# Where the causal mask is applied to the exponentials: mask products on TensorE, or a select on GpSimd, with values in pairs of heads and moved stack reads

## The reference

```python
x = x + attn(layernorm(x), Wq, Wk, Wv, Wo)            # 16 heads of 8, rotary, causal
x = x + xattn(layernorm(x), ctx, W_kv, W_q, W_proj, b) # 16 heads of 8, no mask
x = x + ffn(layernorm(x), gate, w1, b1, w2, b2)        # 8 experts, top 2 per sequence

attn = jnp.einsum('bhqd,bhkd->bhqk', q, k) * scale
attn = jnp.where(causal, -jnp.inf, attn)
attn = jax.nn.softmax(attn, axis=-1)
out = jnp.einsum('bhqk,bhkd->bhqd', attn, v)
```

## Time and profile before

| | |
|---|---|
| median of 3 runs | 200.97 us (200.36 to 201.46) |
| the profiled execution, its own time | 200.95 us |
| its span, first to last instruction | 199.2 us |
| mean granted TensorE clock | 0.947 of 2.4 GHz |
| TensorE busy / VectorE / ACT / GpSimd | 84% / 71% / 53% / 26% of the span |
| TensorE by line, chain that ended last | values L914 11%, second scores L893 9%, first scores L868 8% |
| mask products L898 | 12.1 us busy (overlapping), 48 of them |

### The profile page before, as it was taken

One profiled execution on the slowest core, in us unless ns is written; L12 is line 12 of the kernel. 1 busy time (PEld: TensorE's weight loads), 2 busy tenths in 40 slices (PEclk: granted clock), 3 DMA queues, 4 the chain that ended last, 5 costly groups with the idle time before them and its releaser, 6 DMA issues.

```text
span 199.2 us, 4411 instructions
## 1 busy us (share of the span) xinstructions
PE 166.8 (84%) x1500; PEld 116.1 (58%) x1508; DVE 140.7 (71%) x545; ACT 104.8 (53%) x222; POOL 52.3 (26%) x103
## 2 busy tenths in 40 slices
PE   0686195699599979989998998998998899799994
PEld 0343184485466755755764655654665556598984
DVE  2789299897347899799799889888968346525020
ACT  2132021257147656566566666766676657793451
POOL 7810005668800070030030030010115107126050
PEclk9999669589769999999999999999999999999999
DMA  5817660058227503322321321300340350170720
GB/s 150 238 35 175 164 173 18 3 148 184 70 82 196 184 25 104 110 69 58 109 82 49 98 95 35 90 0 3 113 130 3 100 143 0 17 224 26 229 66 26
DMA packets 23842, 19.05 MB, mean 96 GB/s; under 512 B 2364, under 2 KB 21820, under 8 KB 23100
## 3 DMA queue, kind: packets, MB, share of 16 engines
q1 hardware_dynamic: 22908, 17.79, 31.9%
q10 hardware_dynamic: 912, 0.98, 2.0%
HBM read 12.54 MB, written 2.49 MB: 75 GB/s over the span
## 4 chain that ended last, share of the span: by engine, by line
PE 50%; DVE 19%; DMA 15%; SPq 5%; issue 4%; POOL 3%; ACT 2%; POOLq 0%; DVEq 0%; ACTq 0%
PE psV L914 11%; PE psB L893 9%; PE psA L868 8%; DMA stackQ<-maxT 6%; DMA stackQ<-scratch 4%; DVE masked L623 4%; PE psA L958 4%; PE psM L923 3%; PE psA L975 3%; DMA stackK<-hid 3%; PE psV L975 3%; PE psM L933 3%; DVE stats L554 2%; DVE negmax L629 2%; SPq L402 2%
## 5 line engine op out<-in xcount | busy, mean ns | idle before, releaser
L753 ACT ACTIVATE E<-psB 128x512 f32<-128x512 f32 x112 | 62.3, 595 | 37.3 <-PE psB L893 15.7
L868 PE MATMUL psA<-stackK,stackQ 72*128 72x256 bf16 (+1 forms) x256 | 44.4, 277 | 11.8 <-DMA stackK<-hid 5.5
L893 PE MATMUL psB<-stackQ,stackK 74*128 74x256 bf16 (+1 forms) x256 | 42.2, 264 | 4.6 <-DMA stackQ<-maxT 3.8
L623 DVE CUSTOM_DVE_ANT_0 masked<-psA,row_mask 128x128 bf16<-128x128 f32 (+1 forms) x128 | 36.8, 352 | 11.8 <-PE psA L868 11.7
L629 DVE TENSOR_REDUCE negmax<-psA 128x2 f32<-128x512 f32 x64 | 39.7, 677 | 0.0
L868 PEld LDWEIGHTS psA<-stackK,stackQ 72*128 72x128 bf16 x256 | 23.0, 105 | 21.5 <-DMA stackQ<-scratch 8.6
L914 PE MATMUL psV<-E,V 128*9 128x256 f32 (+1 forms) x512 | 30.9, 359 | 0.2 <-ACT E L753 0.2
L893 PEld LDWEIGHTS psB<-stackQ,stackK 74*128 74x128 bf16 x256 | 22.0, 100 | 12.5 <-DMA stackQ<-maxT 5.6
L468 POOL TENSOR_SCALAR rstd<-mv 128x2 f32<-128x2 f32 x12 | 2.8, 236 | 89.1 <-DVE mv L558 88.9
L914 PEld LDWEIGHTS psV<-E,V 128*9 128x9 f32 x512 | 11.0, 90 | 14.4 <-issue 7.9
L761 ACT ACTIVATE oT<-psV 128x256 f32<-128x256 f32 x32 | 12.3, 384 | 7.9 <-PE psV L914 7.2
(11 more groups left out here) (111 smaller groups left out, 247.0 us busy)
## 6 DMA issues: line engine op xcount, KB each, us to landing
stackK<-scratch SPq DMA_DIRECT2D x18, 192.0 KB
stackQ<-hid SPq DMA_DIRECT2D x36, 64.0 KB
w1s<-w_dram SPq DMA_DIRECT2D x8, 258.0 KB, 2.8
w2s<-w_dram SPq DMA_DIRECT2D x8, 256.0 KB, 3.7
stackQ<-scratch SPq DMA_DIRECT2D x3, 576.0 KB
stackK<-hid SPq DMA_DIRECT2D x18, 64.0 KB
scratch<-hid SPq DMA_DIRECT2D x4, 192.0 KB, 3.7
scratch<-parts_ctx SPq DMA_DIRECT2D x4, 192.0 KB, 4.7
```

The source lines that it names most:

```text
L623: last = dve.tensor_tensor_reduce(out=masked[:, bank, i * keys:(i + 1) * keys], in0=scores[:, i, 0:keys], in1=row_mask[:, S - keys:S], sca ...
L753: act.activation(dst, psB[:, bank].rearrange("p (h q) -> p h q", h=dst.shape[1]), ACT.Exp, scale=SCALE).then_inc(b_taken, 1)
L868: last = pe.matmul(psA[:, bank, i * keys:(i + 1) * keys], stackQ[0:ROWS, b, h, t * P:(t + 1) * P], stackK[0:ROWS, b, h, 0:keys], start=Tru ...
L893: last = pe.matmul(psB[:, bank, i * n:(i + 1) * n], stackK[:, b, h, t * P:(t + 1) * P], stackQ[:, b, h, q0:S], start=(s == 1 or i == 0), s ...
```

## The change

- The mask products of the second pass go, and `mask16T` with them. Instead GpSimd sets the forbidden exponentials to 0 in `E`, two selects per self group: after unit 1 (keys 0 to 127) and after unit 2 (keys 128 to 255), each over 4 heads x 128 columns. The value products wait for both (`e_masked`).
- Values in pairs: heads are grouped as `heads_of(g)`, so two groups that follow each other hold the even and the odd heads of 8. Weights are 18 columns (the head's 9 and 9 zeros, or the reverse), and both groups add into one `psV` without a copy between. ACT copies after each second group; `o_turn` has 4 transposes into one bank, one reciprocal and one product.
- `max_rows` is split: TensorE's transpose (`max_turn`) stays behind the units of its half; VectorE's and SyncE's part (`max_rows`) moves ahead of the units of that half.
- The reads and writes of the stacks are separate steps for keys and queries; those of batch 2 come earlier, those of batch 3 and of the cross keys lie behind the row maxima in SyncE's queue.
- `q_cross`'s split goes from VectorE to an ACT copy and four GpSimd pieces (`q_split`); `k_split` is cut into four steps, a half apart; adding the projection bias is a step of its own (`add_bias`).
- `masked` has 2 buffers instead of 3.

```diff
@@ plan()
+    put(7, "max_turn", 0, 0)
     put(7, "max_rows", 0, 0)
...
-    put(9, "stack_write", 0, 2)
-    put(10, "stack_read", 0, 2)
-    put(14, "stack_write", 0, 3)
+    put(6, "stack_write", 0, 2, 1)
+    put(9, "stack_write", 0, 2, 0)
+    put(9, "stack_read", 0, 2, 1)
+    put(10, "stack_read", 0, 2, 0)
+    put(13, "stack_write", 0, 3, 1)
+    put(14, "stack_write", 0, 3, 0)
+    put(16, "stack_read", 0, 3, 1)
+    put(16, "stack_read", 0, 3, 0)
     for b in range(NB):
-        put(16 + 3 * b, "k_split", 1, b)
-        put(17 + 3 * b, "stack_write_k", 1, b)
+        for n in range(4):
+            put(14 + 4 * b + n, "k_split", 1, b, n)
+        put(17 + 4 * b, "stack_write_k", 1, b)
...
         if j > 0:
-            put(n + 2 * NG, "max_rows", s, b)
-        if j == 1:
-            put(n + 2 * NG + 1, "stack_read", 0, 3)
+            row_of[n + 2 * NG] = (s, b)
...
         if s == 0:
-            put(m, "stack_read_k", 1, b)
+            put(n + 24, "stack_read_k", 1, b)
             put(m + 5, "q_cross", 1, b)
             put(m + 5, "stack_fill", 1, b)
+            for n, later in enumerate((5, 5, 6, 6)):
+                put(m + later, "q_split", 1, b, n)
+            put(m + 7, "add_bias", 1, b)
...
+        if half in row_of:
+            order.append(("max_rows", *row_of[half]))
         order += [step for _, step in sorted(units, key=lambda unit: unit[0])]
+        if half in row_of:
+            order.append(("max_turn", *row_of[half]))
...
+def heads_of(g):
+
+    k, j = divmod(g, 2)
+    return [k * 2 * GH + 2 * i + j for i in range(GH)]
@@ GpSimd
-                    then(pool.memset(mask16T[:, :, :], 0.0))
-                    causal(mask16T, -1)
+                    pool.memset(v_pairs[:, :, VC:2 * VC], 0.0).then_inc(v_init, 1)
...
+                if kind == "scores_exp" and s == 0 and st["u"] >= 1:
+                    pool.wait_ge(b_taken, unit + 1)
+                    t = st["u"] - 1
+                    diagonal = E[:, (job * NG + g) % 3, :, t, t * P:(t + 1) * P]
+                    pool.affine_select(out=diagonal, in_=diagonal, compare_op=ALU.is_ge, fill=0.0, base=0,
+                                       pattern=[[0, GH], [1, P]], channel_multiplier=-1).then_inc(e_masked, 1)
+                if kind == "q_split":
+                    if g == 0:
+                        for bank, k in use[("q_cross", s, b)]:
+                            pool.wait_ge(misc_taken[bank], k)
+                    split(rot[:, b % 2, 0, 0], parts[:, b, 0], parts_q[b], g)
@@ VectorE
-                if kind == "q_cross":
-                    bank, k = misc[0]
...
-                    for t, (bank, k) in enumerate(misc):
-                        dve.wait_ge(misc_full[bank], k)
...
+                    bank, k = misc[0]
+                    dve.wait_ge(misc_full[bank], k)
...
+                    then(dve.reciprocal(r, o[:, :, :, HD]))
@@ ACT
+                if kind == "q_cross":
+                    bank, k = misc[0]
+                    act.wait_ge(misc_full[bank], k)
+                    act.wait_ge(parts_q_self[2 + b] if b < 2 else parts_q[b - 2], NPART)
+                    act.activation(rot[:, b % 2, 0, 0], psM[:, bank, 0:S], ACT.Copy).then_inc(misc_taken[bank], 1)
...
-                if kind == "values":
+                if kind == "values" and g % 2 == 1:
@@ TensorE
-                    if s == 0:
-                        blocks = psB[:, bank].rearrange("p (h q) -> p h q", h=len(heads))[:, :, 0:P]
-                        last = pe.matmul(blocks, ident16[:, :], mask16T[:, 0:len(heads), :], start=False, stop=True,
-                                         skip_group_check=True)
...
-                    else:
-                        pe.wait_ge(v_taken, grp)
+                    elif g % 2 == 0:
+                        pe.wait_ge(v_taken, grp // 2)
...
-                    pe.wait_ge(b_taken, b_units_until(grp))
+                    if s == 0:
+                        pe.wait_ge(e_masked, 2 * (grp + 1))
+                    else:
+                        pe.wait_ge(b_taken, b_units_until(grp))
+                    j = g % 2
...
+                            last = pe.matmul(psV[i * VW:i * VW + 2 * VC, q0:S], V[:, s, b, t, h // 2, j * VC:(j + 2) * VC],
+                                             E[:, grp % 3, i, t, q0:S], start=(j == 0 and t == 0),
+                                             stop=(j == 1 and t == 1), skip_group_check=True,
+                                             tile_position=(0, i * VW))
```

More of the change, by code:

```diff
@@ L53 @@
 VC = HD + 1
+NPAIR = NG // 2
 SCALE = float(HD) ** -0.5
@@ L72, in plan @@
 def plan():
-    extra = {}
+    extra, row_of = {}, {}
     def put(half, *step):
@@ L183, in plan, with unit_of @@
     return steps, a_unit, b_unit
+def heads_of(g):
+    k, j = divmod(g, 2)
+    return [k * 2 * GH + 2 * i + j for i in range(GH)]
+def unit_of(s, g, u):
+    heads = heads_of(g)
+    if s == 0 and u == 0:
+        return heads, 0
+    if s == 0:
+        return heads[2 * (u - 1):2 * u], 1
+    return heads[2 * (u % 2):2 * (u % 2) + 2], u // 2
 def a_units_until(job):
@@ L472, in _ @@
             for st in steps:
-                kind, s, b, g, misc = st["kind"], st["s"], st["b"], st["g"], st["misc"]
+                kind, s, b, g, misc, unit = st["kind"], st["s"], st["b"], st["g"], st["misc"], st["unit"]
+                job = s * NB + b
                 if kind == "ln_stats":
@@ L489, in _ @@
                         then(pool.tensor_tensor(cs, cs, sn, ALU.add))
-                        split(cs, parts[:, b, w], ready)
-                if kind == "q_cross":
+                        for n in range(4):
+                            split(cs, parts[:, b, w], ready, n)
+                if kind == "scores_exp" and s == 0 and st["u"] >= 1:
[9 more added lines that the diff above has]
+                    split(rot[:, b % 2, 0, 0], parts[:, b, 0], parts_q[b], g)
+                if kind == "add_bias":
                     if b == 0:
@@ L498, in _ @@
                 if kind == "k_split":
-                    for bank, k in use[("k_cross", s, b)]:
-                        pool.wait_ge(misc_taken[bank], k)
-                    split(kc[:, b], parts_ctx[:, b], parts_k[b])
+                    if g == 0:
+                        for bank, k in use[("k_cross", s, b)]:
+                            pool.wait_ge(misc_taken[bank], k)
+                    split(kc[:, b], parts_ctx[:, b], parts_k[b], g)
                 if kind == "route":
@@ L619, in _ @@
                             dve.wait_ge(row_mask_set, 1)
-                        if unit >= NA:
-                            dve.wait_ge(a_taken, unit - NA + 1)
-                        for i in range(nh):
-                            last = dve.tensor_tensor_reduce(out=masked[:, bank, i * keys:(i + 1) * keys], in0=scores[:, i, 0:keys],
+                        if unit >= 2:
+                            dve.wait_ge(a_taken, unit - 1)
+                        for i, h in enumerate(heads):
+                            last = dve.tensor_tensor_reduce(out=masked[:, unit % 2, i * keys:(i + 1) * keys], in0=scores[:, i, 0:keys],
                                                             in1=row_mask[:, S - keys:S], scale=-1.0, scalar=LARGEST,
                                                             op0=ALU.add, op1=ALU.min,
-                                                            accum_out=negmax[:, b, h + i, t:t + 1])
+                                                            accum_out=negmax[:, b, h, t:t + 1])
                         last.then_inc(a_taken, 1)
                         continue
-                    dve.tensor_reduce(negmax[:, b, h:h + nh, t], scores, AX_X, ALU.max, negate=True).then_inc(a_taken, 1)
+                    dve.tensor_reduce(negmax[:, b, heads[0]:heads[-1] + 1:2, t], scores, AX_X, ALU.max, negate=True).then_inc(a_taken, 1)
                 if kind == "max_rows":
-                    bank, k = misc[0]
+                    bank, k = use[("max_turn", s, b)][0]
                     dve.wait_ge(misc_full[bank], k)
@@ L860, in _ @@
                         pe.wait_ge(a_taken, unit - NA + 1)
-                    if s == 0 and u == 0:
-                        heads, t, keys = range(g * GH, (g + 1) * GH), 0, P
-                    elif s == 0:
-                        heads, t, keys = range(g * GH + 2 * (u - 1), g * GH + 2 * u), 1, S
-                    else:
-                        heads, t, keys = range(g * GH + 2 * (u % 2), g * GH + 2 * (u % 2) + 2), u // 2, S
+                    heads, t = unit_of(s, g, u)
+                    keys = (t + 1) * P if s == 0 else S
                     for i, h in enumerate(heads):
@@ L917, in _ @@
                     last.then_inc(v_full, 1)
                 if kind == "o_turn":
-                    pe.wait_ge(v_taken, NG * (job + 1))
-                    for t, (bank, k) in enumerate(misc):
-                        misc_free(bank, k)
-                        for i in range(NG):
```

(9 more changed lines are left out.)

132 lines of the change are left out of this document (62 added, 70 removed).

## The result

The changed kernel takes **209.44 us** (median of 4 runs, 206.52 to 214.03) against 201.22 of the kernel before on the same chip: a ratio of 1.029, interval 1.022 to 1.037. Forecast was 196.4, from 191.0 to 202.0, with a chance of 0.16 for slower. The ratio is taken from the faster runs of each kernel, since some runs of both take longer at a lower clock; the medians alone would give 1.041. The sign is wrong, and the time lies outside the range. The profiled execution took 207.13 us, its span is 205.2.

What follows compares the result with a forecast made beforehand. TensorE was taken as the bound, VectorE right behind. From 200.95 us: job 0 0, job 1 -0.9, job 2 -0.3, job 3 -0.7, jobs 4 and 5 -1.5, jobs 6 and 7 -1.2, together -4.6: 196.4, range 191.0 to 202.0.

Steps and rivals of the forecast that it cites:

- 0.5 us a group in which TensorE stands: Groups with selects: TensorE's wait for the select eats the gain of the mask products, 2.79 us where TensorE alone needs 2.29.
- I take the second, 0: Job 0: of clock kept (-1.9 us) or clock falling after the new hole (0 to +1), the latter, priced at 0.
- Mask products removed: TensorE, three products per group in 16 groups: 0.44 us less a group, 7.0 us the most that can come.
- Select 0.60: GpSimd: one select on 4 x 128 fp32 takes 0.60 us, low bound 0.50, high bound 1.1.
- rival B: GpSimd's queue becomes the bound and the kernel slower: 202 us at a select of 1.0, 203.4 at 1.1; chance 0.16.
- Plain group 2.79: Groups with nothing else in them: 2.79 us instead of 2.73, since value products wait for the select.
- Queue ahead of the select: GpSimd: inverse root of the variance puts next value products at v + 4.55; query pieces add 0.75 us in jobs 2 and 3.
- First value products at 48.7: Job 0: first selects stand behind GpSimd's rope work, so the first value products start at 48.7 us instead of 45.43.
- Job 0 without a fall -1.9: Job 0's bound if the clock is kept: two more groups from 52.1 end at 58.4 instead of 60.30.
- Maxima first, pairs, no split on VectorE: Jobs 4 and 5: -0.46 transposes, -0.60 transfer wait, +0.55 VectorE price, about -0.25 query split: -0.76 us each.
- Rival C: Clock stays at 1.2 GHz through job 0 into job 1: 199.4 us; chance 0.15 with what else ends within 1 us.
- Job 3: Now as job 2, then 13.9 + 0.75 = 14.65 us: a gain of 0.7.

## Why the prediction was wrong

**The step that failed** is the pricing of the holes by their length. For jobs 1 to 3 the text has "0.5 us a group in which TensorE stands" and adds waits to TensorE's own times, all at the high clock; the clock was weighed only in job 0 ("I take the second, 0"), there with a fall no longer than the present one. The runs put falls of the clock in its place. With the clock kept up by idle products jobs 1 to 3 take 46.95 us instead of 50.70, and job 0 from its first to its last values 9.61 instead of 14.07: 8.2 of the 15.4 us that the selects cost. In job 0 the fall lasts 13.6 us where the prediction took one no longer than the present one (6.6). A second term was too small as well: the forecast for jobs 1 to 3 was 44.2 us together, and even with the clock at 1.00 they take 46.95, of which the idle products' own time is a part.

**Point by point.**
- *Mask products removed, 7.0 us at most*: seen as a gain in one job of one kernel (13.56 for 14.65), in no whole kernel. With them the kernel is 15.4 us of span shorter.
- *Select 0.60*: 0.638, right; rival B (0.93 and above) is out. The kernel got slower by another way.
- *Plain group 2.79*: 2.95 (64.08 to 67.03), right in kind.
- *Queue ahead of the select*: right in place. The root and the query pieces delay products by 1.78 and 2.05 us (75.27, 84.80). My sum had 4.55 and 4.0 for these groups of job 1, measured 4.80 and 5.00, the second partly at the low clock. In job 2 the first group took 4.53 (80.27 to 84.80) where 2.79 and a part of 1.35 were forecast, at the high clock, and the group with the root 5.91 (89.11 to 95.02) instead of 4.55, at the low clock.
- *First value products at 48.7*: 50.01, since the rope pieces also ended 1.3 later. The next at 52.1, or 53.5 with a fallen clock: 55.14.
- *Job 0 without a fall -1.9*: with products it is -4.7. That bound was too small on the other side too.
- *Maxima first, pairs, no split on VectorE*: jobs 4 to 7 within 0.25 us each, the transfer's wait gone. The price of 0.55 at VectorE's maxima stands in the waits (3.8 us in 4 times, 1.4 in 4 before). But with the maxima behind the units again, and only the order in the queue kept, jobs 4 to 7 are 0.4 us shorter still: being ahead of the units gave nothing, and the order in the queue took most of the transfer's wait away (0.9 us of it is left, 3.8 before).
- *Rival C* had the mechanism that decided, "TensorE now has a hole in every group", and was sized at 3 us from the one fall that the trace of before had. It got too little: 41 us at the low level instead of 21 is, if TensorE does half the work in them, about 10 us, an estimate. Its sign, 0.50 for more than 8 us after 45, came with 27 us.
- *Job 3*: a slip in the sum. The text takes job 3 "as job 2" (15.17), which gives -0.5; -0.7 fits the 15.37 of the trace.

The Trainium skill (TensorE: Matmul & The Clock Gate, Part 1) puts the cost of the low clock at a kernel's start under 1% of a typical span. This trace goes past that, because the clock falls again in the middle: in jobs 1 to 3 alone filling the holes brought 3.75 us, 2% of the span.

**Left open**: why a given fall comes where it does and lasts as long as it does (the same wait of 1.2 us leaves the clock alone in one profile and not in another, and the falls moved from job 0 to jobs 2 to 4 when job 0 was repaired); the clock's exact share, which rests on single profiles; and why idle products before job 0 only moved the fall.

## What to carry to other kernels

If the bounding engine is TensorE and the trace of before shows one fall of its clock after a hole, every new wait of TensorE should be priced twice: by its length, and by the chance of a fall behind it of at least the size seen. Removing work from TensorE was worth nothing here, because the result then had to come through an in-order queue with other work in it; look for what stands ahead of the new step before counting what it frees. Here the best kernel keeps the mask products and takes the rest of the change: 192.02 us, 0.961 of before (0.960 with the maxima behind the units).

## What the runs showed of the hardware

- A select over 128 x 512 takes 638 ns in fp32, against 645 in bf16 of the earlier trace rows.
- The granted clock fell to 0.50 behind waits of TensorE of 1.2 to 3.8 us, whether a select, VectorE, ACT or a transfer ended them, but not behind every such wait. It stayed there for up to 13.6 us in the changed kernel and some 24 with selects alone (49 to 74 us), through stretches in which TensorE was busy without a gap (52 to 54, 60 to 62).
- Kernels with such waits mostly spread: 206.5 to 214.0 us, and 209.3 to 219.1 with selects alone, against 191.6 to 192.4 with mask products. It is no sure sign: selects in groups 1 to 15 gave 205.0 to 206.3, with falls, and mask products with the rows behind 191.4 to 195.5.
